# Coattention of a six-layer decoder: the context's own term of the similarity as a row of its own, copied by ScalarE and added on VectorE

## The reference, cut to what matters

```python
def _L1_xattn_ref(c, q, w_cq, b_cq, w_c, b_c, w_q, b_q, W_l, b_l):
    cq = jnp.einsum('bcd,bqd,d->bcq', c, q, w_cq) + b_cq
    s = (c @ w_c + b_c)[:, :, None] + (q @ w_q + b_q)[:, None, :] + cq
    a = jax.nn.softmax(s, axis=2)
    c2q_att = jnp.einsum('bcq,bqd->bcd', a, q)
    b_att = jax.nn.softmax(jnp.max(s, axis=2), axis=1)
    q2c_att = jnp.einsum('bc,bcd->bd', b_att, c)[:, None, :]
    x = jnp.concatenate([c, c2q_att, c * c2q_att, c * q2c_att], axis=-1)
    z = x @ W_l.T + b_l
    return z

x = x + _L1_xattn_ref(_layernorm(x, axis=-1), ctx_1024, ...)
```

## Time and profile before

| | us |
|---|---|
| median of 3 runs | 2458.41 |
| lowest and highest run | 2455.36, 2462.55 |
| the profiled execution | 2478.62 |
| its span, first to last instruction | 2477.0 |
| coattention's stretch of PE in it | about 1463.8 to 1636.5 |
| TensorE busy over the span | 2116.8 (85%) |

### The profile page before, as it was taken

One profiled execution on the slowest core, in us unless ns is written; L12 is line 12 of the kernel. 1 busy time (PEld: TensorE's weight loads), 2 busy tenths in 40 slices (PEclk: granted clock), 3 DMA queues, 4 the chain that ended last, 5 costly groups with the idle time before them and its releaser, 6 DMA issues. The chain is left out here.

```text
span 2477.0 us, 46573 instructions
## 1 busy us (share of the span) xinstructions
PE 2116.8 (85%) x17286; PEld 1493.3 (60%) x17318; DVE 1540.0 (62%) x3020; ACT 1266.2 (51%) x2039; POOL 1098.8 (44%) x1237
## 2 busy tenths in 40 slices
PE   7699999996995499938989969971899999999995
PEld 5466666654663388725656658851567667676674
DVE  5388888874676665527777836667555554555542
ACT  2366666653342355625565634432565564656642
POOL 2988888830110232145555313310355554555533
PEclk9799999997998699979999969985899999999998
DMA  5000000000002233111011000031344444444423
GB/s 219 1 2 1 0 0 0 0 1 6 8 8 69 89 128 138 77 43 29 26 26 25 1 11 16 15 132 41 109 102 104 98 85 106 97 104 99 90 59 34
DMA packets 62565, 135.99 MB, mean 55 GB/s; under 512 B 10688, under 2 KB 46736, under 8 KB 55568
## 3 DMA queue, kind: packets, MB, share of 16 engines
q0 software_dynamic: 30976, 52.45, 10.5%
q1 hardware_dynamic: 31504, 82.41, 9.4%
HBM read 100.22 MB, written 34.60 MB: 54 GB/s over the span
## 5 line engine op out<-in xcount | busy, mean ns | idle before, releaser
L3245 ACT ACTIVATE f_h<-bank,f_b 128x512 f32<-128x512 f32 x256 | 176.0, 688 | 279.5 <-PE bank L176 272.7
L3282 DVE TENSOR_TENSOR f_hidlo<-f_h,f_hidhi 128x512 f16<-128x512 f32 x256 | 177.4, 693 | 172.5 <-ACT f_hidhi L3246 170.7
L176 PE MATMUL ring<-f_w2hi,f_hidhi 128*128 128x256 f16 x1024 | 279.2, 273 | 6.1 <-DVE f_hidlo L3282 3.8
L176 PE MATMUL ring<-f_w2hi,f_hidlo 128*128 128x256 f16 x1024 | 279.1, 273 | 0.0
L176 PE MATMUL ring<-f_w2lo,f_hidhi 128*128 128x256 f16 x1024 | 279.1, 273 | 0.0
L3336 POOL DMA_INDIRECT out<-f_y,f_to_row x128 | 212.0, 1656 | 47.6 <-issue 34.1
L176 PE MATMUL bank<-f_xthi,f_w1hi 128*128 128x512 f16 x512 | 194.9, 381 | 4.9 <-DVE f_w1lo L3265 4.9
L176 PE MATMUL bank<-f_xtlo,f_w1hi 128*128 128x512 f16 x512 | 194.8, 380 | 0.0
L176 PE MATMUL bank<-f_xthi,f_w1lo 128*128 128x512 f16 x512 | 194.8, 380 | 0.0
L3246 ACT ACTIVATE f_hidhi<-bank,f_b 128x512 f16<-128x512 f32 x256 | 174.2, 680 | 0.0
L3322 POOL DMA_INDIRECT f_xg<-tokens,f_from_row x128 | 148.1, 1157 | 48.1 <-issue 35.6
(11 more groups left out here) (582 smaller groups left out, 5966.5 us busy)
## 6 DMA issues: line engine op xcount, KB each, us to landing
f_raw<-in_e_w SPq DMA_DIRECT2D x32, 1024.0 KB
c_raw<-in_e_w SPq DMA_DIRECT2D x16, 1024.0 KB, 5.9
slots_out<-c_y POOLq DMA_DIRECT2D x8, 640.0 KB, 3.7
x<-in_x SPq DMA_DIRECT2D x1, 4096.0 KB
tokens<-c_xn SPq DMA_DIRECT2D x16, 256.0 KB, 2.6
tokens<-f_xn SPq DMA_DIRECT2D x16, 256.0 KB, 2.5
out<-x SPq DMA_DIRECT2D x1, 4096.0 KB, 14.3
wb<-in_wb SPq DMA_DIRECT2D x1, 3096.0 KB, 33.1
```

Source lines behind the costliest of these rows:

```text
L176: mm = pe.matmul(out, left[a], right[b], start=first and n == 0, stop=last and n == 2)
L3245: act.activation(h32[n % 4][:, :], src, ACT.Gelu_apprx_tanh, bias=bias).then_inc(sig["h_full"], 1)
L3282: dve.tensor_tensor(hid_v[1][:, it, at], h32[n % 4][:, :], hid_v[0][:, it, at], ALU.subtract).then_inc(sig["h_lo"], 1)
```

## The change

The 77 numbers are made once an entry and not once a token tile. PE runs the two products with `e_w_q_wide` at the head of the pair, for both twins, into 77 free columns of bank 1 (`by_context`); they wait for `sim_w_ready` and for the previous pair's `a_t_ready`. ScalarE copies the result to SBUF (`row`) at the head of its own order. The similarity is then only the products with the transposed x, and waits for `row_ready`. VectorE's `tensor_scalar` becomes a `scalar_tensor_tensor`, which adds the bias and the row, the row read twice through a broadcast.

```diff
+            u.by_context = u.bank[1][:, NT * CTX:(NT + 1) * CTX]
...
                     for u in twins:
+                        pe.wait_ge(u["sim_w_ready"], i.now)
+                        pe.wait_ge(u["a_t_ready"], i.before)
+                        for h in range(KT):
+                            mm = pe.matmul(u.by_context, wq_v[:, h, :], u.c_v[:, h, :], start=h == 0, stop=h == KT - 1)
+                        mm.then_inc(u["row_made"], 1)
+                    for u in twins:
                         pe.wait_ge(u["xn_ready"], i.now)
                         pe.wait_ge(u["q2c_read"], i.before)
                         transpose_entry(pe, mem, u.turned, u.xn[q][:, :]).then_inc(u["xn_transposed"], 1)
                     products(0)
                     for u in twins:
                         pe.wait_ge(u["xn_t_ready"], i.now)
-                        pe.wait_ge(u["sim_w_ready"], i.now)
-                        pe.wait_ge(u["a_t_ready"], i.before)
+                        pe.wait_ge(u["row_ready"], i.now)
                         for t in range(NT):
                             out = u.similar[:, t * CTX:(t + 1) * CTX]
                             for h in range(KT):
-                                pe.matmul(out, u.xt_v[q][:, h, t * P:(t + 1) * P], u.sw_v[:, h, :], start=h == 0,
-                                          stop=False)
-                            for h in range(KT):
-                                mm = pe.matmul(out, wq_v[:, h, :], u.c_v[:, h, :], start=False, stop=h == KT - 1)
+                                mm = pe.matmul(out, u.xt_v[q][:, h, t * P:(t + 1) * P], u.sw_v[:, h, :], start=h == 0,
+                                               stop=h == KT - 1)
                         mm.then_inc(u["similar"], 1)
...
                 def pair(q, i, ago, more):
+                    for u in twins:
+                        act.wait_ge(u["row_made"], i.now)
+                        act.wait_ge(u["neg_peak_ready"], i.before)
+                        act.activation(u.row[:, :], u.by_context, ACT.Copy).then_inc(u["row_ready"], 1)
...
                         dve.wait_ge(u["similar"], i.now)
-                        order.step(dve.tensor_scalar(u.a[:, :], u.similar, b_sum[:, :], None, ALU.add))
+                        order.step(dve.scalar_tensor_tensor(out=u.a_v, in0=tiles(u.similar), scalar=b_sum[:, :],
+                                                            in1=u.row[:, :].unsqueeze(1).to_broadcast([P, NT, CTX]),
+                                                            op0=ALU.add, op1=ALU.add))
```

More of the change, by code:

```diff
@@ L2636, in coattention @@
             u.c_t, u.c_n, u.sim_w = sb("c_t", KT * CTX), sb("c_n", D), sb("sim_w", KT * CTX)
-            u.a, u.a_t = sb("a", NT * CTX), sb("a_t", S)
+            u.a, u.a_t, u.row = sb("a", NT * CTX), sb("a_t", S), sb("row", CTX)
             u.neg_peak, u.total = sb("neg_peak", NT), sb("total", NT)
```

## The result

The changed kernel takes 2444.7 us (median of 6 runs, 2441.4 to 2449.1) against 2457.6 us of the kernel before beside it (2455.4 to 2462.6). The medians are 12.9 us apart; the ratio on record over all these runs is 0.9943, with a 95% interval of 0.9932 to 0.9955, which is 14 us less, 11 to 17. Measured twice more, each time beside runs of the kernel before, the changed kernel gave 0.9923 (0.9910 to 0.9937) and 0.9941 (0.9922 to 0.9960). The forecast was 2448.1 us in a range of 2443.5 to 2455.5.

What follows compares the result with a forecast made beforehand. The prediction took TensorE to bound coattention: 7.2 us from fewer groups plus 3.5 from the filled hole, less 0.4 allowed for VectorE, made 10.3 us less, 2448.1 us, in a range of 2443.5 to 2455.5.

Steps and rivals of the forecast that it cites:

- The groups: TensorE's similarity: four groups go and two come each pair, 7.2 us less over all eight pairs.
- The hole: TensorE's gap before a pair's transposes, waiting for q2c's copy; filling it saves 3.5 us over pairs 3 to 8.
- The new groups wait for nothing: At the pair's head on TensorE: their last input, `e_sim_w`, is ready 1.1 us before TensorE comes free.
- The cover before the maxima: VectorE's negated maxima for twin 1 are ready 0.1 to 0.3 us before TensorE's transposes of them.
- rival (a): Before the maxima's transposes: twin 1's maxima come 0.1 to 0.6 us late and eat the hole's gain; about 2452, chance 0.22.
- ScalarE: Two added row copies a pair, 0 to 0.38 us each, hidden at cost 0; without cover 0.8 us a pair.
- VectorE: The new bias-and-row step takes 0.38 us, no change; 0.4 us allowed over all pairs for a slower one.
- rival (b): GpSimd's bias adds block VectorE's new step, losing 1.4 us a pair and all the gain; 2458, chance 0.06.
- Up to the third pair: First two pairs: 1.7 us less in pair 1, 0.1 in pair 2; transposes start 0.27 us later.
- pairs 1 and 2 run at given clocks: In the groups' pricing: pair 1 runs at clock 0.50, and in pair 2 the clock rises in the microsecond from 1490.00.
- More (d): In the first pairs the clock rises 6 us earlier, as the first pair is shorter; 2445 us, chance 0.05.
- Slower (c): In the first pairs the clock rises later; two pairs later the time is 2466 us; chance 0.04.

Runs made afterwards that it cites:

- double_row: The changed kernel with the context's products for the row made twice for each twin; 2452.0 us, ratio to the kernel before 0.9971.
- double_add: The changed kernel with VectorE's add of bias and row issued twice for each twin; 2449.1 us, ratio to the kernel before 0.9963.
- rep_after2: The changed kernel, unedited, profiled a third time; 2447.1 us, ratio to the kernel before 0.9941.
- rep_before2: The kernel before, unedited, profiled a third time; 2460.8 us, ratio 1.0000.
- rep_before: The kernel before, unedited, profiled a second time; 2459.5 us, ratio 1.0002.
- no_row: The changed kernel without the context's groups and row copies, tensor_scalar restored, part of the similarity left out; 2443.7 us, ratio to the kernel before 0.9933.
- rows_late: The changed kernel with the context's groups moved behind both twins' transposes, and ScalarE's row copies behind those of the transposed x; 2453.3 us, ratio 0.9962.
- before: The kernel before, unedited, in its first profile; 2457.6 us, ratio 1.
- split_a: The changed kernel with one product run behind each twin's transposes of the attention weights, not both behind both; 2447.1 us, ratio to the kernel before 0.9951.
- split_warm: The kernel of split_a with 64 unread products on TensorE ahead of the stage's first wait; 2444.0 us, ratio to the kernel before 0.9928.
- q2c_first: The kernel before with VectorE copying q2c before the residual of twin 0, not behind it; 2459.5 us, ratio 0.9999.
- split_a2: The kernel of split_a run and profiled again beside the changed kernel; 2447.6 us, ratio to the kernel before 0.9941.

## Why the prediction was right, and where it was off

- **The bound.** TensorE's own order, with VectorE close behind: right. In double_row more work for TensorE costs its full price, in double_add half of what VectorE was given more shows.
- **The groups.** -1.79 + 0.89 = -0.90 us a pair was forecast. Measured: the similarity went from 3.53 to 1.74 us, the new groups take 0.85; -0.94.
- **The hole.** Forecast at 0.62 and 0.51 us; the step is mis-sized by the time taken for an unhindered follower, 0.90 us, which is 0.86 here (1516.76 to 1517.62). So 0.66 and 0.55. The pair lost 1.59 us where 1.5 was forecast. (The sign "18.5 us a pair" was added up wrongly: 19.9 - 0.9 - 0.6 is 18.4. It came to 18.34.)
- **The new groups wait for nothing.** Right. `e_sim_w` was ready each time.
- **The cover before the maxima.** Forecast 0.07 to 0.32 us, measured 0.15 to 0.33. The allowance of 0.4 us for it was not needed, and rival (a), a wait for `e_neg_peak`, did not come.
- **ScalarE.** 0.236 us a copy, within the bound of 0 to 0.38, and hidden.
- **VectorE.** 0.370 us, forecast 0.38. GpSimd's adds ran over it and did not block it, so rival (b) is out: a step with its source in PSUM beside the row and a bias column in SBUF was not held up as the rule cited there has it for two SBUF inputs.
- **Up to the third pair.** The sum of the terms, 1.8 less 0.27, is 1.5 us and came near to it at like clock (1.2 us). The 42 us named as a sign for the first two pairs were not rightly reckoned: they run from transposes to transposes, and the first pair's new groups stand before its transposes. It was 37.9 us at a clock of 0.82 (rep_after2), against 41.3 in the kernel before (rep_before2), with 2.2 us more between the statistics and the first transposes.
- **The total.** 10.3 us were forecast, 11.0 is what the stage shows at like clock (180.6 to 169.6), and 13 to 19 is what the runs show. The sum itself was good; the rest of the difference was not forecast and is in part luck. The step that did not hold is the sentence that pairs 1 and 2 run at given clocks, pair 1 at 0.50 and the rise of pair 2 fixed in the microsecond from 1490: it was read from one profile with 28.7 us at half clock, where the other two of the same kernel have 18.8 and 19.1. Over 72 executions of the kernel before the mean is 2459.8 us at a mean clock of 0.9296, and a line through them gives 1.3 us for 0.001 of clock; the 17 of the changed kernel have 2444.6 us at 0.9319. Of these 15.2 us some 3.0 go with the clock, 12.2 don't.
- **More (d).** Counted from the stage's statistics, the rise in pair 2 comes about 3 us earlier than in rep_before in two of the three profiles of the changed kernel, and where it was in rep_before2 in the third. That the change itself brings a higher clock was not shown, and the variants speak against the obvious reason, fewer thin float32 groups: double_row, which has two more of them a pair than the changed kernel, ran at 0.9321 on average, no_row, which has none of the new ones, at 0.9288, and rows_late, with the same instructions as the changed kernel, at 0.9286.
- **Slower (c).** Time at half clock in the first pairs does vary, from 15.9 to 28.7 us, but not to the cost of the change. A microsecond of it was priced at 0.47 us; the stage shows less, 3.1 us for 9.9 (before against rep_before) and 4.3 for 12.2 (split_a).

## What to carry to other kernels

Look for work that must be done anyway and waits for nothing, and put it where the bound engine stands in front of a late one: here the place of two groups was worth 0.65 us a pair of the 1.59, and the same work elsewhere cost its full price (18.99 in rows_late against 18.14 without the groups). Measure such a hole from start to start against an unhindered follower, since the bracket shows only a part (0.33 us shown, 0.56 gained). Before taking more from the bound engine, see what is late next; here that was 0.15 to 0.33 us away, and taking the rest of the groups gave 0.2 us of 0.85. And where the gain is under 1% of the time, compare the stage at like clock and set the mean clock beside each total: here 0.001 of it went with 1.3 us.

## What the runs showed of the hardware

The clock's rise in the same program wandered. In the first 54 us of the stage TensorE was at half clock for 28.7, 18.8 and 19.1 us in three profiles of the kernel before, for 15.9, 15.9 and 19.4 in three of the changed one. In the five shorter cases full clock is granted once within the first pair, for 6.8 to 6.9 us, and lost again. In rep_before (busy time by stretch):

```profile
1446.00:1453.00 7.00, 4.73 (x37) 3.68 (x36) 4.22 (x15) 2.53 (x8) 2.53 (x2) 0.99 0.06 14
1453.00:1463.00 10.00, 9.94 (x39) 9.12 (x40) 4.62 (x12) 5.75 (x12) 4.76 (x4) 0.50 0.09 24
```

The first stretch has full clock (2.4 GHz) and the second half clock (1.2 GHz), though TensorE was the busier in the second; the waits of the first pair's softmax lie in the first. By the Trainium skill, "TensorE: Matmul & The Clock Gate", section "Part 1: The HAM clock gate", activity releases the throttled state. split_warm agrees (full clock when the first pair begins, behind 6.5 us of idle products), the second stretch above doesn't, as far as the profile's busy time goes.

Whether the first pair gets that stretch went with the clock before the stage, where no kernel was edited. In the 3 us ahead of the stage's statistics TensorE is idle in all 14 profiles. In eight of them the clock there is 0.50, and all eight have full clock for a while in the first pair; in the other six it is 0.98 to 1.00, and five of these (before, q2c_first, rows_late, no_row, split_a2) stay at 0.50 all through it, only double_row doesn't. So most of the wandering is brought into the stage and not made by the edits; what sets it earlier stays open.

That a `scalar_tensor_tensor` with a source in PSUM, one broadcast in SBUF and a pointer scalar costs no more than a `tensor_scalar` of the same columns (0.370 against 0.378 us), with GpSimd at work beside it, is the other number to keep. GpSimd's add began before it (1521.88 and 1522.52) and ran on.
